# Attention 1 of a two-layer gated block: the exponentials become TensorE's weights, and the maxima a row of the score product that DMA fills

## Chip, cores and metric

One Trainium2 chip, one core. The time is device microseconds of one launch of the whole program, both layers; the runs before gave 1577.19 us (median of three, 1576.49 to 1578.75). Times inside a launch are from one profiled execution, counted from the start of its span. Engines are called as in the profile: PE (TensorE matmuls), PEld (its weight loads), DVE, ACT (ScalarE), POOL (GpSimd), SP (the engine that issues most DMAs).

## What is computed

Two layers, each of a gated attention and a gated feed-forward, on x of 16 x 128 tokens of 256 features. The change is in the second layer's attention ("attention 1"), 32 query heads and 8 groups of keys and values, 8 features a head:

```python
q = (Q @ w_q.T).reshape(B, S, G, HG, HD)
k = (K @ w_k.T).reshape(B, S, G, HD)
v = (V @ w_v.T).reshape(B, S, G, HD)
scores = jnp.einsum('bnghd,bmgd->bnghm', q, k) / scale
scores = jnp.where(pad, NEG_INF, scores)
scores = jnp.where(causal, scores, NEG_INF)
attn = jax.nn.softmax(scores, axis=-1)
out = jnp.einsum('bnghm,bmgd->bnghd', attn, v).reshape(B, S, D)
return out @ w_o.T + b_o
```

x gets tanh(g) times this, and then a mixture of 8 experts follows, whose router reads the result.

## The kernel before

The stages follow each other on all engines: attention 0, feed-forward 0, attention 1, experts. No program sets the order at run time: each engine runs its own list in order, written out by hand with semaphores between the lists.

In feed-forward 0 the keys, values and queries of attention 1 are made beside the main work. Queries and keys are split into three bf16 parts each and sent to DRAM (qsc, ksc); SP loads them back into Q6 and K6 so that 8 features x 6 products of parts lie in 48 rows (two such halves, from row 0 and from row 64, for two heads at once). SP loads K6 early, and Q6 in 48 DMAs of 128 KB, twelve for each quarter of the tokens, at the start of attention 1 (L1468). Values go to VS, each split into an upper and a lower part with a column of ones (18 columns a group): ACT rounds them to VR, DVE takes the difference, POOL copies the upper part.

Attention 1 runs over 16 blocks of 128 tokens, and in each over 4 turns of 2 groups (8 heads): 64 turns i, in a loop over n in which every engine does its part of several turns. In one turn:

- Raw scores (`pe_raw`, L1489 and L1493): two matmuls put the mask into PA, eight add the scores of one bf16 part, tokens on the partitions. DVE takes the maximum over the keys (L1670), 8 numbers a token.
- Shifted scores (`pe_shifted_1`): eight matmuls put the negative maxima into PO by a product with the negative unit matrix (L1503), four of 48 rows and 256 columns add the exact scores (L1510), now with the keys on the partitions.
- ACT takes the exponential (L1623) into P1, POOL clears what lies above the diagonal (L1769), ACT rounds P1 to fp32r (L1629, `act_upper`), DVE takes the rest (L1674, `dve_lower`).
- Weighing (`pe_weigh_1`): four matmuls of 512 columns, with the padded values VP (filled by POOL, L1764) as weights and the exponentials as the moving side, two for each of upper and rest (L1527, L1528); features come out on the partitions.
- Every other turn ACT evicts the sum (L1633), PE turns it to tokens (L1543), DVE adds the parts and divides by the sum of the ones (`dve_normalise`). Once a block PE turns the output (L1549), ACT evicts it (L1639), PE projects it (L1557), DVE adds it to x (L1694, L1699).

For the first 12 blocks, later in the same loop, the router's input is turned (L1574), copied by ACT (L1643) and multiplied with the router's weights (L1582: two matmuls a block, 128x128 fp32 weights, 8 columns). DVE and POOL compute the norms for it at the turns in NEXT, and SP stores the rows (`sp_next_rows`, L1455). At n = 40 SP clears 2 MB of DRAM (eout, L1473). After the loop come the last four blocks' router products, and then the experts (DVE L1995 is their first step).

The order of a turn in PE's list, which decides what waits behind what:

```python
if 0 <= n - 2 < N1:
    pe_shifted_1(pe, n - 2)
if 0 <= n - 4 < N1:
    pe_weigh_1(pe, n - 4)
b = every(n, 4, 11, NB)
if b is not None:
    pe_out_proj(pe, b)
if n < N1:
    pe_raw(pe, n)
```

Of the kernel before, what the change touches and what calls it, by code (L numbers as in the profile page):

```python
# [17 lines left out]
NB = 16  # L18
S = 128
H = 256  # L20
# [46 lines left out]
def build(nc, x, xctxT, maskT, maskrow, small, wqT, wqxT, wkT, wvT, wkvT, smooth, wprojT, gateT, upT, downT, downs,  # L67
# [3 lines left out]
    with ctx:  # L71
# [833 lines left out]
        def pool_attention_0(p):  # L905
# [65 lines left out]
        VS = sb("VS", [128, NB, G, 18])  # L971
# [29 lines left out]
        VR = [sb(f"VR{i}", [128, 256], FR) for i in range(2)]  # L1001
# [15 lines left out]
        s_kk, s_kv, s_ka, s_kr, s_kl, s_kvr, s_klo, s_kvs, s_ks, s_kg = (  # L1017
            sem(n) for n in ("kk", "kv", "ka", "kr", "kl", "kvr", "klo", "kvs", "ks", "kg"))
# [17 lines left out]
        def sp_feed_forward_0(sp):  # L1036
# [65 lines left out]
        def pe_keys_values(pe, q4):  # L1102
# [4 lines left out]
            if q4:  # L1107
                pe.wait_ge(s_kr, q4)
                pe.wait_ge(s_klo, q4)
# [16 lines left out]
        def pe_query_turn(pe, q4):  # L1126
            pe.wait_ge(s_lnorm, layer_norm_count(2, q4))
            if q4 == 0:
                pe.wait_ge(s_kr, 4)
                pe.wait_ge(s_klo, 4)  # L1130
# [57 lines left out]
        def act_keys_values(a, q4):  # L1188
# [8 lines left out]
            if q4 >= 2:  # L1197
                a.wait_ge(s_kvs, q4 - 1)
                a.wait_ge(s_klo, q4 - 1)
            a.activation(VR[q4 % 2][:], PAh[1][:, 0:256], ACT.Copy).then_inc(s_kvr, 1)  # L1200
# [67 lines left out]
        def dve_keys_values(v, q4):  # L1268
            ks = KS[q4 % 2]
            v.wait_ge(s_ka, 2 * q4 + 1)  # L1270
            v.tensor_tensor(RK, PAh[0][0:64, :], ks[:, 0, :], ALU.subtract).then_inc(s_kr, 1)
            v.wait_ge(s_ka, 2 * q4 + 2)
            v.tensor_tensor(ks[:, 2, :], RK, ks[:, 1, :], ALU.subtract).then_inc(s_kl, 1)
            v.wait_ge(s_kvr, q4 + 1)
            if q4 == 0:
                v.wait_ge(s_vone, 2)
            v.tensor_tensor(VS[:, 4 * q4:4 * q4 + 4, :, 9:17], PAh[1][:, 0:256].rearrange("p (b g d) -> p b g d", g=G, d=8),
                            VR[q4 % 2][:].rearrange("p (b g d) -> p b g d", g=G, d=8), ALU.subtract).then_inc(s_klo, 1)
# [91 lines left out]
        def pool_values_upper(p, q4):  # L1370
            p.wait_ge(s_kvr, q4 + 1)
            p.tensor_copy(VS[:, 4 * q4:4 * q4 + 4, :, 0:8], VR[q4 % 2][:].rearrange("p (b g d) -> p b g d", g=G, d=8)).then_inc(
                s_kvs, 1)

# [4 lines left out]
        def pool_feed_forward_0(p):  # L1379
# [4 lines left out]
            for z in range(2):  # L1384
                p.memset(VS[:, :, :, 8 + 9 * z:9 + 9 * z], 1.0 - z).then_inc(s_vone, 1)
# [4 lines left out]
            for q4 in range(4):  # L1390
                pool_values_upper(p, q4)
# [16 lines left out]
        VP = [sb(f"VP{i}", [128, 9, 128], FR) for i in range(2)]  # L1408
        OTS = [sb(f"OTS{i}", [128, 512]) for i in range(2)]
        AO = [sb(f"AO{i}", [128, H]) for i in range(2)]  # L1410
        AOT = sb("AOT", [128, 2, 128])
        OS = sb("OS", [128, 4, 4, 9])
        rl = sb("rl", [128, 4, 4])
        P1 = [sb(f"P1{i}", [128, 1024]) for i in range(2)]
        PH1 = [sb(f"PE1{i}", [128, 2, 512], FR) for i in range(2)]
        PL1 = [sb(f"PL1{i}", [128, 2, 512], FR) for i in range(2)]
        mx1 = [sb(f"mxb{i}", [128, 8], BF16) for i in range(2)]
# [3 lines left out]
        TR = [SS, PC]  # L1421
# [5 lines left out]

        s_wog = sem("wog")
        s_qg = [sem(f"qg{i}") for i in range(4)]
        s_vpz, s_vp, s_sel, s_hi, s_lo, s_ot1, s_oe = (sem(n) for n in ("vpz", "vp", "sel", "hi", "lo", "ot1", "oe"))  # L1430
# [6 lines left out]
        NEXT = {23: 0, 39: 1, 55: 2, 67: 3, 71: 4}  # L1437
# [18 lines left out]

        def sp_attention_1(sp):
# [12 lines left out]
            for n in range(N1 + 14):  # L1470
                if n == 40:
# [7 lines left out]
        def pe_raw(pe, i):  # L1479
            b, g0, tok_ = heads_at(i)  # L1480
            if i == 0:
                pe.wait_ge(s_mask, 1)
                pe.wait_ge(s_kg, 16 * 2 * NP)
# [12 lines left out]

        def pe_shifted_1(pe, i):
            b, g0, tok_ = heads_at(i)
            pe.wait_ge(s_mx, N + i + 1)
            if i:  # L1500
                pe.wait_ge(s_ex, N + i)
            for n in range(8):
                pe.matmul(STB[:, 128 * n:128 * n + 128], mx1[i % 2][:, n:n + 1].broadcast_to([128, 128]), negib[:],  # L1503
                          start=n % 4 == 0, stop=False)
            for half in range(2):
                r = slice(64 * half, 64 * half + 8 * NP)
                for g2 in range(2):
                    g = g0 + g2
                    o = 512 * half + 256 * g2
                    t = pe.matmul(STB[:, o:o + 256], K6[r, g, tok_], Q6[r, 2 * g:2 * g + 2, tok_], start=False, stop=g2 == 1)  # L1510
# [20 lines left out]
        def pe_turn_1(pe, u):  # L1531
            b = u // 2
            pe.wait_ge(s_rt, N + u + 1)
            if u % 2 == 0 and b:
                pe.wait_ge(s_oe, b)
            if u % 2 and b:
                pe.wait_ge(s_add, N + b)
            if u % 2 and b >= 5:
                pe.wait_ge(s_lg, b - 4)
            for j in range(4):  # L1540
                pp, half = divmod(j, 2)
                o = 256 * half + 128 * pp
                t = pe.transpose(TR[u % 2][:, 128 * j:128 * j + 128], OTS[u % 2][:, o:o + 128], identf[:])  # L1543
            t.then_inc(s_T2, 1)

        def pe_out_turn(pe, b):
            pe.wait_ge(s_y0, N + 2 * b + 2)
            for c in range(2):
                t = pe.transpose(TR[0][:, 128 * c:128 * c + 128], AO[b % 2][:, 128 * c:128 * c + 128], identf[:])  # L1549
            t.then_inc(s_ot1, 1)  # L1550

        def pe_out_proj(pe, b):
            pe.wait_ge(s_oe, b + 1)
            if b == 0:
                pe.wait_ge(s_wog, 32)
            for c in range(2):
                t = pe.matmul(TR[1][:, 0:H], AOT[:, c, :], WO[:, c, :], start=c == 0, stop=c == 1)  # L1557
            t.then_inc(s_C, 1)

        def next_bank(b):  # L1560
            return (PAh[0], PAh[1], POa, POb)[b - 12] if b >= 12 else TR[1]
# [23 lines left out]
        def pe_attention_1(pe):  # L1585
            after_feed_forward_0(pe)
            for n in range(N1 + 14):
                b = every(n, 4, 29, NB - 4)
                if b is not None:
                    pe_logits(pe, b)  # L1590
                b = every(n, 4, 10, NB)
                if b is not None:
                    pe_out_turn(pe, b)
                u = every(n, 2, 7, 2 * NB)
                if u is not None:
                    pe_turn_1(pe, u)
                if 0 <= n - 2 < N1:
                    pe_shifted_1(pe, n - 2)
                if 0 <= n - 4 < N1:
                    pe_weigh_1(pe, n - 4)  # L1600
                b = every(n, 4, 11, NB)
# [4 lines left out]
                b = every(n, 4, 28, NB - 4)  # L1606
# [7 lines left out]

        def act_expo_1(a, i):
# [5 lines left out]
            if i >= 2:  # L1621
                a.wait_ge(s_lo, i - 1)
            a.activation(P1[i % 2][:], STB, ACT.Exp, bias=mcf[:, b:b + 1], scale=SC1).then_inc(s_ex, 1)  # L1623

        def act_upper(a, i):
            a.wait_ge(s_sel, i + 1)
            if i >= 2:
                a.wait_ge(s_LO, N + i - 1)
            a.activation(PH1[i % 2][:].rearrange("p a n -> p (a n)"), P1[i % 2][:], ACT.Copy).then_inc(s_hi, 1)  # L1629

        def act_evac_out(a, u):
            a.wait_ge(s_LO, N + 2 * u + 2)
            a.activation(OTS[u % 2][:], OT[u % 2][:], ACT.Copy).then_inc(s_rt, 1)  # L1633

        def act_out_turn(a, b):
# [3 lines left out]
            a.activation(AOT[:].rearrange("p c n -> p (c n)"), TR[0][:, 0:256], ACT.Copy).then_inc(s_oe, 1)  # L1639
# [6 lines left out]
        def act_attention_1(a):  # L1646
            after_feed_forward_0(a)
            for n in range(N1 + 14):
                u = every(n, 2, 6, 2 * NB)
                if u is not None:  # L1650
                    act_evac_out(a, u)
                b = every(n, 4, 10, NB)
                if b is not None:
                    act_out_turn(a, b)
                if 0 <= n - 3 < N1:
                    act_upper(a, n - 3)
                if 0 <= n - 2 < N1:
                    act_expo_1(a, n - 2)
                b = every(n, 4, 28, NB - 4)
# [6 lines left out]
        def dve_maximum_1(v, i):  # L1666
            v.wait_ge(s_S, N + i + 1)
            if i >= 2:
                v.wait_ge(s_ST, N + i - 1)
            v.tensor_reduce(mx1[i % 2][:], PA[:].rearrange("p (j m) -> p j m", m=128), AX, ALU.max).then_inc(s_mx, 1)  # L1670

        def dve_lower(v, i):
            v.wait_ge(s_hi, i + 1)
            v.tensor_tensor(PL1[i % 2][:].rearrange("p a n -> p (a n)"), P1[i % 2][:],  # L1674
# [563 lines left out]
```

## Time and profile before

| | us |
|---|---|
| median of the runs | 1577.19 |
| the profiled execution's own time | 1575.72 |
| its span | 1574.0 |
| TensorE busy in it | 1366.4 (87%) |
| DVE busy | 1215.8 (77%) |
| ACT busy | 1018.8 (65%) |
| POOL busy | 853.1 (54%) |

The mean granted clock of TensorE is 0.957 of full speed. Busy times are sums over the whole span, and each stage has a limit of its own; for a change in one stage the views are cut to that stage: the chain of waits tells which engine's work ended the waiting, the timeline how long a step takes from its start to the start of the next (matmuls overlap, so the busy time of a step is longer than its share), and the windows tell the granted clock and the DMA share of a stretch.

### The profile page before, as it was taken

The page shows a single profiled execution, that of the slowest core. Times are in us where ns is not written, and L with a number is a line of the kernel's source. Part 1 is how long each engine was busy: PE and PEld are TensorE (multiplying, and loading weights), DVE is VectorE, ACT ScalarE, POOL GpSimd, SP SyncE. Part 2 cuts the span into 40 slices and gives each one's busy share as a digit, 9 for nine tenths or more (in the row PEclk, how much of TensorE's full clock was granted, in tenths as well). Part 3 has the DMA queues.
Part 4 walks back from the last instruction along what each step waited for, and adds up shares of the span by engine and source line. Part 5 has one row for each costly group of instructions (what it writes and reads, how often), then busy time and mean ns, then how long its engine had stood idle before and what let it go on. Part 6 is the DMA issues. An engine that isn't in the chain of part 4 may idle for free. (4 is left out here: it accounts for less than half of the span.)

```text
span 1574.0 us, 30371 instructions
## 1 busy us (share of the span) xinstructions
PE 1366.4 (87%) x11712; PEld 1173.5 (75%) x11712; DVE 1215.8 (77%) x2318; ACT 1018.8 (65%) x2168; POOL 853.1 (54%) x912
## 2 busy tenths in 40 slices
PE   0356999999999999999999996999769898994995
PEld 0356899999999999999999985676536555553995
DVE  7999888888888888888888797633448988886554
ACT  4687677877777777778777774312136665652773
POOL 2688767667677676676775464101114433341673
PEclk9999999999999999999999998999979998995997
DMA  3100000000100000001001002340254002003563
GB/s 102 37 24 28 15 22 15 15 21 15 35 15 14 22 15 15 22 15 35 3 14 51 2 1 78 77 62 21 57 97 74 15 1 68 1 15 132 182 216 127
DMA packets 62239, 69.85 MB, mean 44 GB/s; under 512 B 5424, under 2 KB 54800, under 8 KB 61968
## 3 DMA queue, kind: packets, MB, share of 16 engines
q1 hardware_dynamic: 59488, 60.54, 14.6%
q0 software_dynamic: 2432, 7.34, 1.4%
q8 instruction: 93, 1.52, 0.4%
q14 instruction: 50, 0.41, 0.1%
q10 hardware_dynamic: 176, 0.04, 0.0%
HBM read 55.56 MB, written 12.34 MB: 43 GB/s over the span
## 5 line engine op out<-in xcount | busy, mean ns | idle before, releaser
L903 POOL TENSOR_TENSOR RB<-YS,M 128x512 bf16<-128x512 f32 x128 | 151.8, 1186 | 180.3 <-DVE YS L753 180.3
L579 ACT ACTIVATE QT<-B,sm 128x256 f32<-128x256 f32 x256 | 130.4, 560 | 163.8 <-PE B L435 163.8
L1769 POOL TENSOR_SCALAR_AFFINE_SELECT P<-P 128x1024 f32<-128x1024 f32 x64 | 82.1, 1282 | 154.7 <-ACT P L1623 154.7
L455 PE MATMUL SS<-QT,KT 128*128 128x256 f32 x512 | 154.8, 397 | 11.4 <-DVE mx L714 11.3
L892 POOL TENSOR_TENSOR yy<-vv,half 128x12 f32<-128x12 f32 x64 | 147.8, 2310 | 5.3
L403 PE MATMUL PA<-WH,XQ 128*128 128x256 f32 x512 | 140.2, 305 | 7.0 <-ACT SQ L608 7.0
L733 DVE TENSOR_TENSOR QN<-QN,yy 128x512 f32<-128x512 f32 x128 | 134.1, 1048 | 1.7 <-POOL yy L892 1.5
L714 DVE TENSOR_REDUCE mx<-SS 128x4 bf16<-128x512 f32 x128 | 88.2, 689 | 60.7 <-PE SS L447 59.7
L405 PE MATMUL PA<-WL,XQ 128*128 128x256 f32 x512 | 128.8, 283 | 0.0
L726 DVE TENSOR_REDUCE vv<-SQ 128x6 f32<-128x768 f32 x128 | 120.6, 942 | 0.0
L435 PE MATMUL B<-identf,QN 128*128 128x128 f32 x768 | 105.5, 274 | 6.4 <-ACT LNT L534 6.4
L1629 ACT ACTIVATE PE<-P 128x1024 fp32r<-128x1024 f32 x64 | 67.7, 1058 | 65.1 <-POOL P L1769 65.1
L423 PE MATMUL PA<-W,XB 128*128 128x128 bf16 x1536 | 109.2, 221 | 0.4 <-POOL XB L833 0.4
L403 PEld LDWEIGHTS PA<-WH,XQ 128*128 128x128 f32 x512 | 98.6, 193 | 7.6 <-ACT SQ L608 7.6
L471 PE MATMUL PO<-V,PPP 128*128 128x129 f32 x512 | 98.9, 275 | 5.2 <-DVE Y L741 5.2
L582 ACT ACTIVATE KT<-B,sm 128x128 f32<-128x128 f32 x256 | 103.1, 460 | 0.0
L471 PE MATMUL PO<-VR,PPP 128*128 128x129 f32 x512 | 99.0, 275 | 0.0
L405 PEld LDWEIGHTS PA<-WL,XQ 128*128 128x128 f32 x512 | 98.8, 193 | 0.0
L899 POOL TENSOR_TENSOR VR<-V,RSM 128x256 f32<-128x256 f32 x128 | 96.6, 754 | 0.0
L489 PE MATMUL PC<-PH,RT 128*128 128x256 f32 x512 | 92.0, 301 | 3.1 <-ACT RT L600 2.8
L435 PEld LDWEIGHTS B<-identf,QN 128*128 128x128 f32 x768 | 88.5, 141 | 6.6 <-issue 6.6
L753 DVE SCALAR_TENSOR_TENSOR YS<-Y,M 128x512 f32<-128x512 bf16 x128 | 89.3, 697 | 4.4
(331 smaller groups left out, 4516.1 us busy)
## 6 DMA issues: line engine op xcount, KB each, us to landing
W<-in_w SPq DMA_DIRECT2D x16, 1024.0 KB
Q<-qsc SPq DMA_DIRECT2D x48, 128.0 KB
WR<-in_wprojT SPq DMA_DIRECT2D x16, 256.0 KB, 3.0
K<-ksc SPq DMA_DIRECT2D x12, 256.0 KB
qsc<-T POOLq DMA_DIRECT2D x8, 384.0 KB, 4.2
X<-in_x SPq DMA_DIRECT2D x4, 512.0 KB, 5.9
CR<-in_xctxT SPq DMA_DIRECT2D x8, 256.0 KB, 2.8
RSM<-rsm_d SPq DMA_DIRECT2D x16, 128.0 KB, 4.1
```

The source lines that it names most:

```text
L403: pe.matmul(PA[:, 256 * k:256 * k + 256], XQ[:, k, c, bs], wh[:, c, 256 * k:256 * k + 256], start=c == 0, stop=False)
L405: t = pe.matmul(PA[:, 256 * k:256 * k + 256], XQ[:, k, c, bs], wl[:, c, 256 * k:256 * k + 256], start=False, stop=c == 1)
L423: t = pe.matmul(PA[:, 768 + 128 * k:896 + 128 * k], XB[:, k, c, bs], wb[:, c, part, 128 * k:128 * k + 128], start=c == 0 and part == 0, st ...
L435: t = pe.transpose(dst, QN[i % 4][:, 128 * h:128 * h + 128], identf[:])
L455: pe.matmul(SS[:, 256 * z:256 * z + 256], k[:, 128 * z:128 * z + 128], q[:, 256 * z:256 * z + 256], start=True, stop=False)
L471: t = pe.matmul(PO[:, z, 129 * j:129 * j + 129], p[:, 128 * h:128 * h + 128], v[j][:, 1 - z, :], start=True, stop=True)
L579: a.activation(QT[i % 2][:, o:o + 256], B1[:, o:o + 256], ACT.Identity, bias=col(n + "b"), scale=col(n + "w"))
L582: t = a.activation(KT[i % 2][:, o:o + 128], B2[:, o:o + 128], ACT.Identity, bias=col(n + "b"), scale=col(n + "w"))
L726: v.tensor_reduce(w_[:, 6 * h:6 * h + 6], SQ[:].rearrange("p (h d) -> p h d", d=128), AX, ALU.add).then_inc(s_red, 1)
L733: v.tensor_tensor(q[:, 0:4], q[:, 0:4], y[:, 6 * h:6 * h + 4].unsqueeze(2).broadcast_to([128, 4, 128]), ALU.mult).then_inc(s_mul, 1)
L892: p.tensor_tensor(yy[j % 2][:], v_, half[:], ALU.pow).then_inc(s_rstd, 1)
L903: p.tensor_tensor(RB[i % 2][:], YS[:], M[:], ALU.subtract).then_inc(s_rb, 1)
```

## The change

- The maxima of the four turns of a block are kept together (mxb, 32 columns); one matmul turns and negates them (`pe_max_turn`), ACT copies them to MT, and two DMAs of SP write them into row 48 of each half of Q6 (`sp_maxima`). Row 48 of K6 holds ones, written in feed-forward 0 by two DMAs. The shifted scores are now four matmuls of 49 rows, without the eight of L1503.
- The exponentials stay fp32, are not split, and are the weights of the weighing: eight matmuls a turn, each with 128x128 fp32 weights and 9 columns of values (8 features and the ones). They give the output by tokens, so the eviction and turns of L1633 and L1543 go; DVE divides straight from PSUM, once a block.
- The values are not split: ACT writes them to VS; the difference on DVE and the copies on POOL go, and so do VP and its clearing.
- P1 has three buffers. Turns are drawn apart: shifted scores of turn i come 7 turns of the loop after its raw scores (2 before), the weighing 2 after that; the output, router and norm steps move 4 turns later.

```diff
         def sp_feed_forward_0(sp):
...
             sp.wait_ge(s_ks, 64)
+            sp.wait_ge(s_vone, 2)
             for half in range(2):
+                sp.dma_start(K6[64 * half + 48:64 * half + 49, :, :].rearrange("o g (b t) -> o (g b) t", t=128),
+                             ones1[:]).then_inc(s_kg, 16)
...
-        NEXT = {23: 0, 39: 1, 55: 2, 67: 3, 71: 4}
+        NEXT = {27: 0, 43: 1, 59: 2, 71: 3, 75: 4}
...
+        def sp_maxima(sp, b):
+            sp.wait_ge(s_mte, b + 1)
+            for half in range(2):
+                sp.dma_start(Q6[64 * half + 48:64 * half + 49, :, 128 * b:128 * b + 128],
+                             MT[b % 2][16 * half:16 * half + 16, :]).then_inc(s_mr[b % 2], 16)
...
         def sp_attention_1(sp):
...
                         sp.dma_start(Q6[r0:r0 + 8, :, 512 * q4:512 * q4 + 512], src[:, :, 512 * q4:512 * q4 + 512]).then_inc(
                             s_qg[q4], 16)
             for n in range(N1 + 14):
+                b = every(n, 4, 5, NB)
+                if b is not None:
+                    sp_maxima(sp, b)
...
+        def pe_max_turn(pe, b):
+            pe.wait_ge(s_mx, N + 4 * b + 4)
+            if b:
+                pe.wait_ge(s_mte, b)
+            if b >= 3:
+                pe.wait_ge(s_oe, b - 2)
+            pe.matmul(SS[0:32, 256:384], mxb[b % 2][:], negib[:], start=True, stop=True).then_inc(s_mt, 1)
...
         def pe_shifted_1(pe, i):
             b, g0, tok_ = heads_at(i)
-            pe.wait_ge(s_mx, N + i + 1)
+            if i % 4 == 0:
+                pe.wait_ge(s_mr[b % 2], 32 * (b // 2 + 1))
             if i:
                 pe.wait_ge(s_ex, N + i)
-            for n in range(8):
-                pe.matmul(STB[:, 128 * n:128 * n + 128], mx1[i % 2][:, n:n + 1].broadcast_to([128, 128]), negib[:],
-                          start=n % 4 == 0, stop=False)
             for half in range(2):
-                r = slice(64 * half, 64 * half + 8 * NP)
+                r = slice(64 * half, 64 * half + 8 * NP + 1)
...
         def pe_weigh_1(pe, i):
             b, g0, tok_ = heads_at(i)
-            u = i // 2
-            ps_ = OT[u % 2]
-            vp = VP[b % 2][:].rearrange("p g n -> p (g n)")
-            pe.wait_ge(s_lo, i + 1)
-            if i % 4 == 0:
-                pe.wait_ge(s_vp, b + 1)
-            if u >= 2 and i % 2 == 0:
-                pe.wait_ge(s_rt, N + u - 1)
-            for g2 in range(2):
+            pe.wait_ge(s_sel, i + 1)
+            if i % 4 == 0 and b >= 2:
+                pe.wait_ge(s_y0, N + b - 1)
+            for n in range(8):
+                half, g2, pp = n // 4, n // 2 % 2, n % 2
                 g = g0 + g2
-                o = 128 * (g + 1) - 32 * (g % 4)
-                n = slice(256 * g2, 256 * g2 + 256)
-                pe.matmul(ps_[:], vp[:, o:o + 128], PH1[i % 2][:, :, n], start=g % 4 == 0, stop=False)
-                t = pe.matmul(ps_[:], vp[:, o:o + 128], PL1[i % 2][:, :, n], start=False, stop=g % 4 == 3)
+                o = 9 * (4 * g + 2 * pp + half)
+                t = pe.matmul(OT[b % 2][:, o:o + 9], P1[i % 3][:, 128 * n:128 * n + 128], VS[:, b, g, :], start=True, stop=True)
             t.then_inc(s_LO, 1)
...
         def pe_attention_1(pe):
             after_feed_forward_0(pe)
             for n in range(N1 + 14):
...
+                b = every(n, 4, 5, NB)
+                if b is not None:
+                    pe_max_turn(pe, b)
+                if 0 <= n - 7 < N1:
+                    pe_shifted_1(pe, n - 7)
+                if 0 <= n - 9 < N1:
+                    pe_weigh_1(pe, n - 9)
...
         def act_expo_1(a, i):
...
-            if i >= 2:
-                a.wait_ge(s_lo, i - 1)
-            a.activation(P1[i % 2][:], STB, ACT.Exp, bias=mcf[:, b:b + 1], scale=SC1).then_inc(s_ex, 1)
+            if i >= 3:
+                a.wait_ge(s_LO, N + i - 2)
+            a.activation(P1[i % 3][:], STB, ACT.Exp, bias=mcf[:, b:b + 1], scale=SC1).then_inc(s_ex, 1)
...
-        def act_upper(a, i):
...
-        def act_evac_out(a, u):
...
-        def dve_lower(v, i):
...
-        def pool_values(p, b):
...
```

## Rows read from the trace of the kernel before

**Rows 1.** The page's first line.

```profile
span 1574.0 us, 30371 instructions
```

**Rows 2.** Timeline, PE, stage ends: start us, us, what, [idle before <-releaser].

```profile
1155.85 1.01 PE L1489 MATMUL PA<-MS,identb 128*128 128x512 bf16 x2 [10.28 <-DMA Q<-qsc]
...
1158.76 1.04 PE L1489 MATMUL PA<-MS,identb 128*128 128x512 bf16 x2 [1.34 <-DVE mxb L1670]
...
1160.27 1.03 PE L1503 MATMUL PO<-negib,mxb 128*128 128x128 bf16 x8
1161.24 0.61 PE L1510 MATMUL PO<-Q,K 48*128 48x256 bf16 x4
1161.78 1.04 PE L1489 MATMUL PA<-MS,identb 128*128 128x512 bf16 x2
...
1436.64 1.83 PEld L1582 LDWEIGHTS PA<-WG,ZX 128*128 128x128 f32 x8
1438.36 1.83 PEld L1582 LDWEIGHTS PO<-WG,ZX 128*128 128x128 f32 x8
```

**Rows 3.** The same, the last weighing matmul and the experts' first step.

```profile
1419.72 0.40 PE L1528 MATMUL B<-PL,VP 128*128 128x512 f32 x1
...
1440.52 0.29 DVE L1995 TENSOR_REDUCE rm<-LG 128x16 f32<-128x128 f32 x1
```

**Rows 4.** Windows, mid-stage: stretch, us, busy (count) by engine, PEclk, DMA share, GB/s.

```profile
1212.00:1421.00 209.00, 183.90 (x1504) 116.46 (x1502) 172.82 (x287) 124.78 (x148) 79.78 (x104) 0.94 0.06 19
```

**Rows 5.** Chain that ended last, in order of time: start us, us, what.

```profile
1196.70 1.10 ACT P L1623
...
1197.86 1.34 POOL P L1769
...
1199.25 0.94 issue
1200.19 1.10 ACT P L1623
```

**Rows 6.** Timeline of PE in mid-stage, at a granted clock of 1.00.

```profile
1282.45 0.60 PE L1489 MATMUL PA<-MS,identb 128*128 128x512 bf16 x2
...
1283.33 0.66 PE L1543 MATMUL SS<-identf,OTS 128*128 128x128 f32 x4
...
1284.37 0.40 PE L1510 MATMUL PO<-Q,K 48*128 48x256 bf16 x4
1284.69 0.50 PE L1527 MATMUL B<-PE,VP 128*128 128x512 f32 x1
...
1285.72 1.03 PE L1557 MATMUL PC<-WO,AOT 128*128 128x256 f32 x4
...
1291.19 0.61 PE L1582 MATMUL PC<-WG,ZX 128*128 128x8 f32 x4 [0.47 <-ACT ZX L1643]
```

**Rows 7.** Groups, 1155 to 1425: xcount | busy us, mean ns | idle before.

```profile
L1670 DVE TENSOR_REDUCE mxb<-PA 128x8 bf16<-128x1024 f32 x64 | 78.1, 1220 | 18.2 <-PE PA L1493 17.5
```

**Rows 8.** SP issues in the timeline; a window; a DMA with us to landing.

```profile
1127.95 75.89 SPq L1468 DMA_DIRECT2D Q<-qsc  x48
...
1210.00:1212.00 2.00, 1.74 (x15) 0.78 (x14) 2.00 (x3) 1.48 (x2) 0.45 (x1) 1.00 0.19 47
...
WG<-in_wgate SPq DMA_DIRECT2D x1, 8.0 KB, 2.9
```

**Rows 9.** Timeline of the weight loads, one block's router product.

```profile
1291.19 0.52 PEld L1582 LDWEIGHTS PC<-WG,ZX 128*128 128x128 f32 x4 [0.71 <-ACT ZX L1643]
```

**Rows 10.** Windows (columns as in rows 4), four stretches of attention 1.

```profile
1158.00:1170.00 12.00, 9.90 (x68) 4.81 (x69) 5.54 (x6) 5.58 (x6) 2.49 (x3) 0.50 0.56 88
1170.00:1180.00 10.00, 10.00 (x86) 5.78 (x84) 8.07 (x10) 6.76 (x8) 3.44 (x3) 0.94 0.56 71
1436.60:1440.30 3.70, 3.68 (x18) 3.58 (x17) 0.50 (x3) 0.64 (x2) 0.00 (x0) 0.50 0.12 40
...
1240.00:1260.00 20.00, 15.44 (x134) 9.41 (x134) 17.58 (x25) 10.14 (x13) 10.66 (x18) 1.00 0.08 27
```

More of the change, by code:

```diff
@@ L1383, in pool_feed_forward_0 @@
             pool_parts(p, 1)
-            for z in range(2):
-                p.memset(VS[:, :, :, 8 + 9 * z:9 + 9 * z], 1.0 - z).then_inc(s_vone, 1)
+            p.memset(VS[:, :, :, 8:9], 1.0).then_inc(s_vone, 1)
+            p.memset(ones1[:], 1.0).then_inc(s_vone, 1)
             p.memset(caus[:], 0.0).then_inc(*ps.up())
@@ L1407, in build @@
         WG = sb("WG", [128, 2, E])
-        VP = [sb(f"VP{i}", [128, 9, 128], FR) for i in range(2)]
-        OTS = [sb(f"OTS{i}", [128, 512]) for i in range(2)]
         AO = [sb(f"AO{i}", [128, H]) for i in range(2)]
         AOT = sb("AOT", [128, 2, 128])
[L1412 to L1417, printed above, removed]
+        rl = sb("rl", [128, 32])
+        P1 = [sb(f"P1{i}", [128, 1024]) for i in range(3)]
+        mxb = [sb(f"mxb{i}", [128, 32], BF16) for i in range(2)]
+        MT = [sb(f"MT{i}", [32, 128], BF16) for i in range(2)]
         ti = sb("ti", [128, 128], I32)
@@ L1429, in build @@
         s_qg = [sem(f"qg{i}") for i in range(4)]
[L1430 removed]
+        s_sel, s_ot1, s_oe = (sem(n) for n in ("sel", "ot1", "oe"))
+        s_mt, s_mte = sem("mt"), sem("mte")
+        s_mr = [sem("mr0"), sem("mr1")]
         s_nt, s_xt, s_lgp, s_lg, s_zr = (sem(n) for n in ("nt", "xt", "lgp", "lg", "zr"))
@@ L1509, in pe_shifted_1 @@
                     o = 512 * half + 256 * g2
-                    t = pe.matmul(STB[:, o:o + 256], K6[r, g, tok_], Q6[r, 2 * g:2 * g + 2, tok_], start=False, stop=g2 == 1)
+                    t = pe.matmul(STB[:, o:o + 256], K6[r, g, tok_], Q6[r, 2 * g:2 * g + 2, tok_], start=True, stop=True)
             t.then_inc(s_ST, 1)
@@ L1555, in pe_out_proj @@
                 pe.wait_ge(s_wog, 32)
+            else:
+                pe.wait_ge(s_add, N + b)
+            if b >= 5:
+                pe.wait_ge(s_lg, b - 4)
             for c in range(2):
-                t = pe.matmul(TR[1][:, 0:H], AOT[:, c, :], WO[:, c, :], start=c == 0, stop=c == 1)
+                t = pe.matmul(PC[:, 0:H], AOT[:, c, :], WO[:, c, :], start=c == 0, stop=c == 1)
             t.then_inc(s_C, 1)
         def next_bank(b):
-            return (PAh[0], PAh[1], POa, POb)[b - 12] if b >= 12 else TR[1]
+            return (PAh[0], PAh[1], POa, POb)[b - 12] if b >= 12 else PC
         def pe_next_turn(pe, b):
@@ L1587, in pe_attention_1 @@
             for n in range(N1 + 14):
-                b = every(n, 4, 29, NB - 4)
+                b = every(n, 4, 33, NB - 4)
                 if b is not None:
                     pe_logits(pe, b)
-                b = every(n, 4, 10, NB)
+                b = every(n, 4, 14, NB)
                 if b is not None:
                     pe_out_turn(pe, b)
[L1594 to L1601, printed above, removed]
+                b = every(n, 4, 5, NB)
[5 more added lines that the diff above has]
+                    pe_weigh_1(pe, n - 9)
+                b = every(n, 4, 15, NB)
                 if b is not None:
@@ L1605, in pe_attention_1 @@
                     pe_raw(pe, n)
-                b = every(n, 4, 28, NB - 4)
+                b = every(n, 4, 32, NB - 4)
                 if b is not None:
@@ L1648, in act_attention_1 @@
             for n in range(N1 + 14):
[L1649 to L1652, printed above, removed]
+                b = every(n, 4, 5, NB)
+                if b is not None:
+                    act_max_turned(a, b)
+                b = every(n, 4, 14, NB)
                 if b is not None:
                     act_out_turn(a, b)
[L1655 to L1659, printed above, removed]
+                if 0 <= n - 7 < N1:
+                    act_expo_1(a, n - 7)
+                b = every(n, 4, 32, NB - 4)
                 if b is not None:
@@ L1735, in dve_attention_1 @@
                     dve_routing_constants(v)
-                b = every(n, 4, 29, NB - 4)
+                b = every(n, 4, 33, NB - 4)
                 if b is not None:
                     dve_logits(v, b)
-                u = every(n, 2, 7, 2 * NB)
-                if u is not None:
-                    dve_normalise(v, u)
-                if 0 <= n - 3 < N1:
-                    dve_lower(v, n - 3)
-                b = every(n, 4, 11, NB)
+                b = every(n, 4, 13, NB)
+                if b is not None:
+                    dve_normalise(v, b)
+                b = every(n, 4, 15, NB)
                 if b is not None:
@@ L1787, in pool_attention_1 @@
                     pool_routing_constants(p)
-                b = every(n, 4, 0, NB)
-                if b is not None:
-                    pool_values(p, b)
-                if 0 <= n - 2 < N1:
-                    pool_select(p, n - 2)
+                if 0 <= n - 7 < N1:
+                    pool_select(p, n - 7)
                 if n in NEXT and NEXT[n] <= 2:
@@ L1826, in build @@
         who = (B2[:, 0:3 * E], PC[:, 0:3 * E])
-        s_slots, s_sub, s_exp, s_oh, s_A, s_who, s_idx, s_wgt = (
-            sem(n) for n in ("slots", "sub", "exp", "oh", "A", "who", "idx", "wgt"))
+        s_slots, s_sub, s_exp, s_oh, s_A, s_who, s_idx, s_wgt, s_hi = (
+            sem(n) for n in ("slots", "sub", "exp", "oh", "A", "who", "idx", "wgt", "hi"))
         s_e = [sem("e0"), sem("e1")]
```

117 lines of the change are left out of this document (38 added, 79 removed).

## The prediction

> **What bounds the kernel now.** I read the page's head first [rows 1]: the profiled execution has a span of 1574.0 us and a time of 1575.72, so 1.7 us lie around the span; the median of the runs, 1577.19, is 1.5 above it. The change touches attention 1, which runs from 1155.85 (the first score matmul, held back by the Q loads) [rows 2] to 1440.5, where the experts begin [rows 3]. In its middle TensorE is busy for 183.90 of 209 us at a granted clock of 0.94 [rows 4]: nearly full, but the chain of waits [rows 5] shows who sets the pace. An exponential (1.10) ends, POOL's causal select (1.34) follows, then ScalarE's rounding copy, in front of the next exponential in its program, holds that back for another 0.94 (the chain calls it "issue"). From exponential to exponential that is 3.49 us (1196.70 to 1200.19), 64 times. The last weighing matmul ends at 1420.1; the tail to the experts takes 20.4 us [rows 3].
>
> **What goes.** The rounding copy leaves ScalarE, the subtraction leaves DVE, and PE loses the eight matmuls that put the maxima into the scores, the four weighing matmuls (1.03 us, 1284.69 to 1285.72) and the turns of L1543, 0.66 us every other turn [rows 6]. The 3.49 us chain is gone: exponential and select now lie between a score matmul and a weighing two turns later, so at least 2 x 3 us of PE work cover their 2.5 us. DVE keeps one maximum of 1.22 us a turn [rows 7], covered by the 2.2 us of PE work that stand between one raw score and the next. What replaces the chain is PE's own sum and the way of the maxima through DMA.
>
> **The preparation** in feed-forward 0 loses casts and subtractions and gains two DMAs of ones, issued with the K loads, long ahead of their use; the gate and up matmuls, which PE runs meanwhile, cover both, and the clearing of VP falls into the wait for the Q loads. If that cover were gone it would be a few copies. I take 0, with bounds of 2 us either way.
>
> **The first maxima.** SP issues 48 Q loads first, from 1127.95 without a break for 75.89 us, thus until 1203.84; the maxima's DMAs stand behind them in SP's program and in its queue, whose data runs on: the share of the DMA engines is still 0.19 in 1210 to 1212 [rows 8]. Before, the first shifted score started at 1160.27 [rows 2]. Now PE does seven raw scores (n = 0 to 6, done by about 1176 at the 2.91 us from 1155.85 to 1158.76) and waits at shifted score 0. If the small transfers overtook the Q data, they would land at 1203.84 + 2.9 (the nearest small one, 8 KB) = 1207; if they wait behind it, at 1212 or up to 2.9 later. I take 1212.5: the queue is the same. Later maxima have two turns (6 us or more) for a ScalarE copy, two issues and such a landing; only b = 9, behind the 2 MB clearing of eout, could be late, by 0 to 3 us once. I take 0. SP's other waits come after the maxima of their turn.
>
> **PE's sum at full clock.** Raw scores 0.88 (1282.45 to 1283.33), shifted scores 0.32 (1284.37 to 1284.69; the 49th row adds no column) [rows 6]. The weighing is new: eight matmuls of fp32 weights with nine columns. Its nearest relative is the router product, 128x8 with fp32 weights: two matmuls of the program give four records, each with its own weight load, and the four loads take 0.52 together [rows 9], 0.13 each with the first one's beginning; half of the step at half clock (0.215, below) is 0.11, which I take. So 16 loads: 16 x 0.11 and 0.12 to begin = 1.9 us a turn, bound by the loads. From shifted score 0 to the last weighing: 64 x (0.32 + 1.9) = 142; 57 raw scores x 0.88 = 50; 16 x (output turn 0.3, half of L1543's; maxima 0.1, an estimate from one matmul of 128 columns; projection 0.9 of the 1.03 shown, whose end the next covers) = 21; 12 blocks of router work x 1.4 (turn 0.3, wait 0.47, logits 0.61) = 17 [rows 6]. Sum 230.
>
> **PE's sum at half clock.** At the granted clock of 0.50 (1.2 GHz instead of 2.4) the raw scores took 1.51 (1158.76 to 1160.27), the shifted ones 0.54 (1161.24 to 1161.78), and eight such loads start 1.72 after the eight before, a step of 0.215 [rows 2]: 16 x 0.215 + 0.2 = 3.6. 64 x (0.54 + 3.6) = 265; 57 x 1.51 = 86; the rest at twice the full price or a little less, 16 x 2.5 and 12 x 2.0, 64. Sum 415.
>
> **Which of the two.** After the long wait PE begins at half clock. Rows show that being busy does not bring the full clock by itself: from 1158 to 1170 PE was busy 9.90 of 12 us with raw, maxima and shifted scores and stayed at 0.50, and from 1436.6 to 1440.3 it was busy 3.68 of 3.70 with weight loads and eight-column matmuls, the very form of the new weighing, and stayed at 0.50 [rows 10]. In the first stretch the clock rose only after the 512-column weighing matmuls had joined (0.94 from 1170 on); the change takes those and the maxima matmuls away and fills their place with loads. So I take half clock almost throughout, with short rises where the projection (four records of 256 columns) and raw scores stand together, some 8% of the way: 415 - 0.08 x 185 = 400 us. The bounds are 230 and 415.
>
> The page "TensorE: Matmul & The Clock Gate" of the Trainium skill ("Why this matters for your kernels") says that an engine kept continuously busy with matmuls gets the full rate. By that rule the sum would be 230 instead of 400, the first rival below; the stretch at 1436.6, busy without gaps at 0.50, speaks against it.
>
> **The sum.** 1212.5 + 400 = 1612.5 for the last weighing. Tail: 20.4 less an eviction and two small DVE steps, which are gone: 18, bounds 16 and 21. Experts unchanged: 1574.0 - 1440.5 = 133.5. Span 1764, time 1765.7, and with the 1.5 of the median 1767: slower by 190 us, of which 52 lie before shifted score 0 (1212.5 instead of 1160.3), part of them won back by the seven raw scores done ahead.
>
> **Rivals.** (A) The clock comes back and stays: PE is never idle after 1212.5. For it: 1240 to 1260 shows 1.00 although PE was busy only 15.44 of 20 us [rows 10]. Against it: the rows at 0.50 above, and PE starts from 0.50. It gives 1212.5 + 230 + 18 + 133.5 + 3.2 = 1597, slower by 20, since the wait for the maxima isn't won back. (B) It comes and goes: raised at each projection and held for a turn or more, so that a third to a half of the work runs at full clock. With 415 - 0.33 x 185 = 354 to 415 - 0.5 x 185 = 322 it gives 1721 to 1690. (C) Faster: at full clock the weight loads overlap each other, so that the weighing is bound by something shorter. At the step of the bf16 matmuls of 128 columns (eight between 1160.27 and 1161.24 [rows 2], 0.12 each at half clock, so 0.06 at full) 16 records take 1.1 with their beginning instead of 1.9: 64 x 0.8 = 51 less, 1546. It decides from the point where PE's way is under 1420.1 - 1212.5 + 2.4 = 210 us, that is, a step under 0.09. Against it: four loads in a row at 0.13 or a little less, with nothing else to wait for [rows 9], and it needs the full clock too. That the maxima's row does not do its work has no sign in the diff: the row of ones in K6 and the negative maxima in Q6 are both there.
>
> **How the numbers follow.** Half clock 0.72, A 0.12, B 0.12, C 0.03, and 0.01 for no change. The likeliest gives 1767; its own range is 1735 (rises for a quarter of the way) to 1790 (no rise, latest landing, late transfers). The range reaches down through B, to 1685, and up to 1795; A and C are left out with 0.16. A measurement here tells about 0.2%, 3 us, from no change. Faster 0.03, same 0.01, slower 0.96.
>
> **What would show it.** In the trace after: PE idle until about 1212 with shifted score 0 released by the DMA of the maxima; 16 weight loads a turn at a step of 0.21 (right) or 0.11 (A); the granted clock near 0.50 in attention 1; exponentials 6 us apart or more, with ScalarE, DVE and POOL idle most of the time; the router's start near 1630. It would be wrong if the first shifted score started before 1200, or if the clock stood at 1.00 in the middle of the stage.

## The result, and the profile after

The median of four runs went from 1577.97 to 1743.68 us. One of the four of the changed kernel, 1763.04, was in a slower state with a lower granted clock, so the ratio, 1.1014 (95% interval 1.0976 to 1.1052), and all differences between medians below leave such runs out; the median of the other three is 1739.61. The prediction was 1767, with a range of 1685 to 1795. The profiled run took 1747.76 us, the slowest of these three.

The page of the changed kernel first: its span, the granted clock over 40 slices, and the groups of attention 1 (busy us, mean ns, idle before).

```profile
span 1745.7 us, 30282 instructions
...
PEclk9889999999999999999999899955555555555798
...
L1525 PEld LDWEIGHTS B<-VS,P 128*128 128x128 f32 x1024 | 215.1, 319 | 24.8 <-issue 24.6
L1729 POOL TENSOR_SCALAR_AFFINE_SELECT P<-P 128x1024 f32<-128x1024 f32 x64 | 69.9, 1094 | 329.5 <-ACT P L1618 329.5
L1525 PE MATMUL B<-VS,P 128*128 128x9 f32 x1024 | 220.7, 355 | 0.0
...
L1654 DVE TENSOR_REDUCE mxb<-PA 128x8 bf16<-128x1024 f32 x64 | 78.3, 1224 | 222.1 <-PE PA L1490 222.1
...
L1618 ACT ACTIVATE P<-PO,mcf 128x1024 f32<-128x1024 f32 x64 | 71.2, 1113 | 166.6 <-PE PO L1513 166.6
```

DVE and ScalarE now wait for TensorE, and POOL for ScalarE's exponential (222, 167 and 330 us idle ahead of their main steps), and the clock line has a run of fives where attention 1 lies. The windows show it closer (stretch, us, busy by engine, PEclk, DMA share, GB/s).

```profile
1160.00:1180.00 20.00, 8.69 (x60) 2.81 (x59) 7.34 (x6) 0.27 (x1) 0.00 (x0) 0.50 0.55 101
1180.00:1200.00 20.00, 0.00 (x0) 0.00 (x0) 0.00 (x0) 0.00 (x0) 0.00 (x0) 0.50 0.56 110
...
1240.00:1300.00 60.00, 60.00 (x310) 43.03 (x311) 16.14 (x20) 11.80 (x14) 9.82 (x9) 0.50 0.00 1
1300.00:1350.00 50.00, 49.19 (x264) 35.98 (x264) 17.61 (x32) 10.83 (x13) 12.07 (x21) 0.53 0.04 11
1350.00:1450.00 100.00, 98.11 (x502) 71.33 (x502) 28.90 (x54) 20.83 (x27) 19.91 (x34) 0.50 0.09 27
1450.00:1550.00 100.00, 96.93 (x539) 70.74 (x540) 30.13 (x51) 21.94 (x28) 19.85 (x28) 0.57 0.02 6
```

From 1180 to 1200 nothing computes; from 1240 to 1300 TensorE is busy without a gap and has half its clock. The timeline gives the steps behind both.

```profile
1150.40 42.18 SPq L1462 DMA_DIRECT2D Q<-qsc  x30
1156.01 1.01 PE L1486 MATMUL PA<-MS,identb 128*128 128x512 bf16 x2 [10.81 <-DMA Q<-qsc]
...
1175.22 1.22 DVE L1654 TENSOR_REDUCE mxb<-PA 128x8 bf16<-128x1024 f32 x1 [1.70 <-PE PA L1490]
1192.62 17.57 SPq L1448 DMA_DIRECT2D Q<-MT  x4
1203.19 0.61 PE L1513 MATMUL PO<-Q,K 49*128 49x256 bf16 x4 [28.03 <-DMA Q<-MT]
...
1240.81 1.01 PE L1486 MATMUL PA<-MS,identb 128*128 128x512 bf16 x2
...
1242.30 0.61 PE L1513 MATMUL PO<-Q,K 49*128 49x256 bf16 x4
1242.84 3.58 PE L1525 MATMUL B<-VS,P 128*128 128x9 f32 x16
1246.27 2.05 PE L1546 MATMUL PC<-WO,AOT 128*128 128x256 f32 x4
...
1454.09 1.95 PE L1525 MATMUL B<-VS,P 128*128 128x9 f32 x16
1455.90 0.59 PE L1486 MATMUL PA<-MS,identb 128*128 128x512 bf16 x2
...
1592.49 3.42 PE L1525 MATMUL B<-VS,P 128*128 128x9 f32 x16
...
1610.92 0.29 DVE L1952 TENSOR_REDUCE rm<-LG 128x16 f32<-128x128 f32 x1
```

Seven raw scores are done at 1175; the first shifted score starts at 1203.19, after 28.03 us of idle time that the maxima's DMA ends (before: 1160.27 [rows 2]). A weighing takes 3.43 us (1242.84 to 1246.27), a plain turn 5.46. At 1454 the clock is up for a moment, and the same sixteen records take 1.81.

Where the 171.7 us of span come from: the first shifted score is 42.9 later; from it to the last weighing's end it takes 392.7 (1203.19 to 1595.91) in place of 259.8 (1160.27 to 1420.1 [rows 2, 3]), 132.9 more; the tail is 5.4 shorter (15.0), the experts 1.3 longer.

### The profile page after: what moved, and what is told of

The parts are those of the page before. It is cut to its first block and busy times, and to the rows that moved or that the text cites. A ratio compares the mean times of both kernels' runs of the same rounds, so it can differ in the third digit from the quotient of the medians.

```text
span 1745.7 us, 30282 instructions
## 1 busy us (share of the span) xinstructions
PE 1530.3 (88%) x11856; PEld 1318.9 (76%) x11856; DVE 1112.1 (64%) x2152; ACT 945.1 (54%) x2088; POOL 828.5 (47%) x892
## 5 line engine op out<-in xcount | busy, mean ns | idle before, releaser
L1525 PEld LDWEIGHTS B<-VS,P 128*128 128x128 f32 x1024 | 215.1, 319 | 24.8 <-issue 24.6
L1729 POOL TENSOR_SCALAR_AFFINE_SELECT P<-P 128x1024 f32<-128x1024 f32 x64 | 69.9, 1094 | 329.5 <-ACT P L1618 329.5
L1525 PE MATMUL B<-VS,P 128*128 128x9 f32 x1024 | 220.7, 355 | 0.0
L1654 DVE TENSOR_REDUCE mxb<-PA 128x8 bf16<-128x1024 f32 x64 | 78.3, 1224 | 222.1 <-PE PA L1490 222.1
L1618 ACT ACTIVATE P<-PO,mcf 128x1024 f32<-128x1024 f32 x64 | 71.2, 1113 | 166.6 <-PE PO L1513 166.6
```

The source lines that it names most:

```text
L1525: t = pe.matmul(OT[b % 2][:, o:o + 9], P1[i % 3][:, 128 * n:128 * n + 128], VS[:, b, g, :], start=True, stop=True)
```

## The experiments

The theory: two costs that add. The maxima stand behind 48 query loads on SP, and the new weighing leaves TensorE at half clock. Times are medians; ratios are to the kernel before, run beside each. In the cuts of code "..." stands for lines left out.

**Query loads interleaved with the maxima** (`sp_queries` issues the twelve loads of one quarter).

```diff
-            for q4 in range(4):
...
+            sp_queries(sp, 0)
             for n in range(N1 + 14):
                 b = every(n, 4, 5, NB)
                 if b is not None:
                     sp_maxima(sp, b)
+                    if b < 3:
+                        sp_queries(sp, b + 1)
```

> Only the order of SP's issues is changed: the query loads of the second, third and fourth quarter go out behind the maxima of blocks 0, 1 and 2, not ahead of them. Theory (two costs that add: TensorE idles 28 us for the first maxima, which stand behind 48 query loads on SP; and the new weighing then leaves it at half clock): the first shifted score comes right behind the seventh raw score, at about 1177 us in place of 1203, the granted clock stays 0.50 for most of the stage, and the time falls by about 26 us, from 1744 to about 1718. Rival (the idle stretch is what puts the clock at half, and a stage without it would run up): the clock rises to 1.00 and the time is near 1580. Second rival (the wait only moves to the first turn of the second quarter, which now waits for its loads): no change, 1744.

Measured: 1726.36, ratio 1.0968 (1.0929 to 1.1008), 13 us less than the changed kernel, half of the expected 26; the clock stayed at 0.50 from 1240 to 1300. Its timeline:

```profile
1167.83 8.34 SPq L1457 DMA_DIRECT2D Q<-qsc  x12
...
1171.72 0.61 PE L1517 MATMUL PO<-Q,K 49*128 49x256 bf16 x4
...
1197.28 0.61 PE L1517 MATMUL PO<-Q,K 49*128 49x256 bf16 x4 [8.50 <-DMA Q<-MT]
```

The first shifted score comes at 1171.72, without a wait, 31.5 us sooner. Block 1's maxima now stand behind the twelve loads of the second quarter, and TensorE waits 8.50 us for them: the second rival, in part. The profiled spans differ by 24.3. So the order on SP is the cause of the long wait, and the idle stretch isn't what sets the clock.

**The maxima's DMAs issued by ACT.**

```diff
+            a.wait_ge(s_mte, b + 1)
+            for half in range(2):
+                a.dma_start(Q6[64 * half + 48:64 * half + 49, :, 128 * b:128 * b + 128],
+                            MT[b % 2][16 * half:16 * half + 16, :]).then_inc(s_mr[b % 2], 16)
```

> The query loads stay in their order; only the two DMAs of each block's maxima are issued by ACT, behind its own copy, in place of SP. Theory (the 28 us come from SP's order, in which the maxima stand behind 48 query loads): the maxima of block 0 go out at about 1170 us, the first shifted score comes at about 1177 in place of 1203, with no later wait for block 1, and the time falls by 24 to 28 us to about 1718. Rival (what holds the maxima is the transfers themselves, since both share the 16 DMA engines): they are issued early and land when the query loads are through, the first shifted score stays at 1195 to 1203 and the time at 1735 to 1744.

Measured: 1719.51, ratio 1.0888 (1.0852 to 1.0924), 20 us less, or 28.6 between the profiled spans. Its timeline:

```profile
1167.69 22.11 SPq L1462 DMA_DIRECT2D Q<-qsc  x20
...
1169.13 1.24 ACTq L1608 DMA_DIRECT2D Q<-MT  x2
...
1177.28 0.61 PE L1510 MATMUL PO<-Q,K 49*128 49x256 bf16 x4 [2.92 <-DMA Q<-MT]
```

The maxima go out 23.5 us sooner, while some twenty query loads are still to be issued, and release the score 8.2 us later: 2.92 us idle in place of 28.03. What held the maxima was their place on SP. The loads beside them still cost something: from issue to landing the maxima took up to 7.5 us here, up to 9.4 behind the loads on SP, and 1.7 and 1.8 in the medians over all blocks. So nearly all of the gain is the earlier issue. The page "DMA: Bandwidth & Descriptors" of the Trainium skill ("Queues, rings and completion order") says that SP and ACT own separate queue rows, between which a DMA engine takes turns. The separate rows agree with this run; the turns it doesn't show, since the landing is little shorter than behind the loads.

**Weighing over 112 columns.**

```diff
-                t = pe.matmul(OT[b % 2][:, o:o + 9], P1[i % 3][:, 128 * n:128 * n + 128], VS[:, b, g, :], start=True, stop=True)
+                c = 72 * b + 9 * g
+                w = min(112, 72 * NB - c)
+                t = pe.matmul(OT[b % 2][:, o:o + w], P1[i % 3][:, 128 * n:128 * n + 128], vs_[:, c:c + w], start=True, stop=True)
```

> The weighing's eight matmuls a turn go over 112 columns in place of 9: the same weights, the same loads, the same results in the 9 columns that are read; the other columns are overwritten by the next heads or lie past the 288 that are read. Theory (the clock stays at half because the weighing shows TensorE nine columns between two loads of fp32 weights): the granted clock goes to 1.00 for most of the stage, the weighing takes about 1.8 to 2.0 us a turn, as in the short rises of the changed kernel, a turn about 3.1 us, and the time falls from 1744 to about 1600 (1585 to 1625); the start's wait of 28 us stays. Rival (the clock is at half for another reason, such as the idle start or the loads themselves, and the columns don't matter): the clock stays 0.50 and the time is 1744 or, where the columns outlast the loads, longer, up to 1780.

Measured: 1618.54, ratio 1.0271 (1.0242 to 1.03), 121 us less. Windows and a turn from its timeline:

```profile
1200.00:1220.00 20.00, 13.97 (x79) 9.02 (x80) 3.67 (x3) 6.00 (x6) 4.37 (x4) 0.50 0.09 17
1220.00:1240.00 20.00, 20.00 (x190) 15.09 (x190) 8.86 (x10) 7.28 (x8) 6.18 (x6) 1.00 0.01 1
1240.00:1300.00 60.00, 57.96 (x524) 43.06 (x522) 31.19 (x48) 20.62 (x25) 20.13 (x29) 0.97 0.03 11
```

```profile
1220.04 0.60 PE L1486 MATMUL PA<-MS,identb 128*128 128x512 bf16 x2
...
1221.23 2.04 PE L1529 MATMUL B<-VS,P 128*128 128x112 f32 x16
1223.11 0.60 PE L1486 MATMUL PA<-MS,identb 128*128 128x512 bf16 x2
```

The same weights and loads (their order by heads changed too, which wasn't tried alone), with columns that nobody reads, and the clock goes to 1.00 some 15 us after the first shifted score (1204.97). The weighing takes 1.88 us, hardly more than the 1.81 of the nine columns at full clock: the loads set its length either way. A turn falls from 5.46 to 3.07 us. This is the larger cost, and it is the clock's.

**A burst ahead of the first shifted score.**

```diff
+            if i == 0:
+                for _ in range(24):
+                    pe.matmul(STB[:, 0:512], identb[:], MS[:, 0, :].unsqueeze(1).broadcast_to([128, 4, 128]), start=True, stop=True)
```

> Ahead of the first shifted score, behind its wait, TensorE does 24 more bf16 matmuls of 512 columns into the bank that the score then overwrites; nothing else is changed. Theory (it is the steady stream of weighings that the chip answers with half clock): the clock rises in or behind the burst and is back at 0.50 within a few turns, and the time is 1744 plus 5 to 10 us for the burst less at most 2.4 us for each turn at full clock, 1740 to 1755. Rival (the stage only starts low, after 28 us of idle, and would hold full clock once raised): the clock stays 1.00 to the end and the time is about 1595 to 1610.

Measured: 1747.6, ratio 1.1088 (1.1029 to 1.1146), 8 us more. Its timeline:

```profile
1198.35 7.25 PE L1508 MATMUL PO<-MS,identb 128*128 128x512 bf16 x24 [24.87 <-DMA Q<-MT]
1205.54 0.40 PE L1516 MATMUL PO<-Q,K 49*128 49x256 bf16 x4
...
1208.51 0.40 PE L1516 MATMUL PO<-Q,K 49*128 49x256 bf16 x4 [1.70 <-ACT P L1621]
1208.84 0.86 PE L1486 MATMUL PA<-MS,identb 128*128 128x512 bf16 x2
...
1210.93 3.58 PE L1528 MATMUL B<-VS,P 128*128 128x9 f32 x16
```

The burst brings full clock (0.40 for a shifted score), and it is gone in the second raw score, 0.86, ahead of the first weighing, 3.58. TensorE had waited 1.70 us for the first exponential between; from there on it is busy without a gap (1220 to 1300), and the clock stays at 0.50. So a raised clock isn't held. Whether the wait or the work behind it took the clock away, this run doesn't tell, as it was gone before any weighing; the next run shows a fall without a wait.

**The maxima by matmuls again, the new weighing kept.** Where the 49th row was, eight matmuls of `mxb` columns against `negib` as in the kernel before; no turn, copy or DMA of maxima.

> The change's other half alone is undone: the maxima enter the score product by eight 128-column bf16 matmuls a turn, as in the kernel before, with 48 rows of queries and keys; no turn of the maxima and no DMA of them (their columns lie in three buffers, so that the lag of seven turns holds). The weighing by fp32 weights over 9 columns stays. Theory: the start's wait of 28 us goes, and eight matmuls a turn come, some 0.9 us at half clock (0.5 at full). If the weighing alone decides the clock it stays at 0.50 and the time is 1744 - 28 + 64 x 0.9 = about 1770 (1750 to 1785). Rival (the 1024 bf16 columns that come back each turn are enough for the clock to rise): 1.00 for most of the stage, a turn near 3.6 us, and a time of about 1744 - 28 - 64 x 1.9 = 1595.

Measured: 1765.3, ratio 1.1176 (1.1144 to 1.1209). Its windows, one stretch, and a rise in its timeline:

```profile
1240.00:1300.00 60.00, 60.00 (x356) 44.74 (x356) 14.21 (x17) 10.79 (x11) 9.89 (x10) 0.53 0.00 1
```

```profile
1251.40 0.62 PE L1506 MATMUL PO<-negib,mxb 128*128 128x128 bf16 x8
...
1252.28 1.95 PE L1525 MATMUL B<-VS,P 128*128 128x9 f32 x16
...
1255.08 1.03 PE L1506 MATMUL PO<-negib,mxb 128*128 128x128 bf16 x8
```

The 1024 bf16 columns that come back each turn hardly raise the clock. It rises behind a projection (at 1248), stays up for one weighing, and falls (0.62 to 1.03 for the same eight matmuls) with no idle time between. So the halves of the change part: the new weighing, with its order of turns, makes the kernel 12% slower, and the maxima's row takes 26 us of that back although its first DMA stalls TensorE for 28.

**Both costs away: 112 columns, and two query loads a turn between the maxima.**

```diff
+                k = 2 * (n - 5)
+                if 0 <= k < 36:
+                    sp.wait_ge(s_mx, N + n + 1)
+                    sp_queries(sp, 1 + k // 12, range(k % 12, k % 12 + 2))
```

> Both costs taken away at once: the weighing goes over 112 columns, and SP issues only the first quarter's query loads ahead of the loop, then each block's maxima in their place, and two query loads a turn between them. Theory (the two costs are separate and add): the first shifted score at about 1172 us, the granted clock 1.00 from some 15 us behind it, and the profiled span of the run with 112 columns alone (1608.0) falls by 31 us to about 1577, the time to 1575 to 1590, level with the kernel before. Rival (they are not separate: with the loads running beside the scores, the DMAs or TensorE are slower, or a late query load stops TensorE): 1595 to 1615.

Measured: 1592.9, ratio 1.0079 (1.0049 to 1.011), outside the expected 1575 to 1590. Its timeline, then its windows:

```profile
1172.86 9.39 SPq L1457 DMA_DIRECT2D Q<-qsc  x8
...
1182.29 1.14 SPq L1448 DMA_DIRECT2D Q<-MT  x2
...
1192.93 0.61 PE L1519 MATMUL PO<-Q,K 49*128 49x256 bf16 x4 [4.32 <-DMA Q<-MT]
```

```profile
1212.00:1400.00 188.00, 172.80 (x1426) 130.51 (x1424) 79.29 (x130) 58.40 (x73) 53.86 (x75) 0.90 0.17 31
```

The maxima of block 1 are issued behind eight loads and release their score 10.6 us later: TensorE still waits for maxima behind the few loads ahead of them, from 1190 to 1425 for 16.5 us in all, and the clock is 0.90 (0.94 with 112 columns alone). That is the rival's case, with maxima late and not query loads.

**The same with a burst ahead of the first raw score** (24 matmuls as above, while the first query loads land).

> As the run with both costs taken away, and in the idle time ahead of the first raw score, while the first quarter's query loads land, TensorE does 24 bf16 matmuls of 512 columns into a bank that the first raw score overwrites. Theory: the idle time of 6 to 10 us covers most of the 24, the clock is at 1.00 when the raw scores start and stays there, each of the first seven raw turns takes about 2.3 in place of 2.92 us and the first turns behind them 3.1 in place of 5.5, so 5 to 15 us less than the run with both: 1565 to 1580. Rival (the clock falls back in the first raw turns, which are idle for nearly half of their time): no difference from that run, or some us more where the 24 outlast the idle time.

Measured: 1596.86, ratio 1.0106 (1.0078 to 1.0133): no gain. Its timeline:

```profile
1159.17 0.60 PE L1494 MATMUL PA<-MS,identb 128*128 128x512 bf16 x2 [1.34 <-DVE mxb L1666]
...
1161.46 1.04 PE L1494 MATMUL PA<-MS,identb 128*128 128x512 bf16 x2 [1.34 <-DVE mxb L1666]
```

The rival held: three raw turns run at full clock, the fourth is at half again.

**112 columns and ACT's queue.**

> The run with the maxima's DMAs issued by ACT and the run with 112 columns together: query loads in their first order and at full speed ahead of the scores, no wait for block 1, weighing over 112 columns. Theory (two separate costs, and the paced order gave some of its gain back in later waits and slower turns): the run with 112 columns alone, 1618.5 us, less the 24 us that ACT's queue brought, 1594, or somewhat less: 1585 to 1598. Rival (the costs are not separate): no better than the paced run, 1593 to 1610.

Measured: 1576.53, ratio 0.9992 (0.9962 to 1.0022): the kernel before's time, and 22 us better than the two gains added. Its windows:

```profile
1212.00:1400.00 188.00, 178.81 (x1603) 134.66 (x1602) 92.44 (x158) 65.13 (x82) 61.55 (x92) 0.98 0.07 21
```

The first shifted score starts at 1180.33, 24.6 us sooner than with 112 columns alone, as ACT's queue promised. From there to the end of the last weighing it takes 243.8 in place of 252.2 us, and the clock goes with that: 0.98 here, 0.94 there in the same stretch. Another 7 us are in no trace, since the profiled spans differ by 35 and the medians by 42. Its own runs lie between 1566.94 and 1589.58; why the clock falls once more or once less isn't settled.

**The mask's matmuls left out as well.**

```diff
-            for half in range(2):
-                pe.matmul(PAh[half], identb[:], MS[:, b, :].unsqueeze(1).broadcast_to([128, 4, 128]), start=True, stop=False)
...
-                              start=False, stop=n % 4 == 3)
+                              start=True, stop=True)
```

> As the run with ACT's queue and 112 columns, and the two 512-column bf16 matmuls that put the mask into each raw score are left out: the maxima then go over all 128 keys of the block, hidden ones too; the hidden ones still get no weight, since the select and the exponential's bias stay. Theory (TensorE is the bound of the changed stage, so what it no longer does is gained): 0.53 us a turn at full clock, 64 turns, 34 us: about 1558 (1550 to 1575), faster than the kernel before. Rival (these 1024 columns a turn are among those that hold the clock up): the clock falls in a good part of the stage, and the time is 1594 to 1660.

Measured: 1562.79, ratio 0.9893 (0.9844 to 0.9942), 14 us less than with the mask, and 1.1% faster than the kernel before, which wasn't run without its mask. A turn of its timeline, and a window:

```profile
1288.26 0.41 PE L1485 MATMUL PA<-K,Q 8*128 8x128 bf16 x8
...
1290.89 0.41 PE L1485 MATMUL PA<-K,Q 8*128 8x128 bf16 x8
```

```profile
1240.00:1400.00 160.00, 148.15 (x1264) 120.26 (x1262) 76.86 (x140) 56.60 (x72) 53.90 (x85) 0.89 0.08 25
```

A turn at full clock is 2.63 in place of 3.07 us, which by itself would bring 64 x 0.44 = 28 us. In the profiled executions the first shifted score comes 6.5 us sooner, and from it to the last weighing, with 57 such turns (25 us), it takes 236.0 in place of 243.8, only 7.8 less. Some 7 us of the rest are longer waits of TensorE (19.6 in place of 12.5); the others go with the clock, 0.89 where the run with the mask has 0.98 in the same stretch. So the theory and the rival both hold in part.

**The first seven raw turns filled** (ACT's queue, 112 columns, with the mask).

```diff
+                if n < 7:
+                    for _ in range(3):
+                        pe.matmul(STB[:, 0:512], identb[:], MS[:, 0, :].unsqueeze(1).broadcast_to([128, 4, 128]), start=True, stop=True)
```

> As the run with ACT's queue and 112 columns, and behind each of the first seven raw scores, where TensorE waits 1.3 us a turn for the maximum, it does three bf16 matmuls of 512 columns into the bank that the first shifted score overwrites. Theory: with no idle time the clock is at 1.00 within the first raw turns and stays there into the weighing; raw turns of 2.3 in place of 2.92 us and two to four weighing turns of 3.1 in place of 5.5 bring 5 to 12 us against the run without them. Rival (the wait of 3 us for the first maxima lets the clock fall anyway): 0 to 3 us.

Measured: 1572.08, ratio 0.9971 (0.9948 to 0.9994), 4.3 us less than without the filling; the two intervals overlap. Its timeline:

```profile
1161.65 0.82 PE L1598 MATMUL PO<-MS,identb 128*128 128x512 bf16 x3
...
1172.93 0.61 PE L1510 MATMUL PO<-Q,K 49*128 49x256 bf16 x4 [3.61 <-DMA Q<-MT]
...
1178.94 3.64 PE L1526 MATMUL B<-VS,P 128*128 128x112 f32 x16
```

Full clock in the raw turns from the third on, half again behind 3.61 us of idle time: mostly the rival.

**Without the mask and with the filling.**

> The run without the mask's matmuls and the run with the first seven raw turns filled, together (ACT's queue and 112 columns in both). Theory (their gains lie in different places, one in every turn, one ahead of the first weighings): 1562.8 us less the 4.5 us that the filling brought, about 1558 (1552 to 1564), faster than the kernel before. Rival (without the mask's columns the clock falls more often, and the filling holds it up only at the start): no different from the run without the filling, 1560 to 1566.

Measured: 1564.3, ratio 0.9885 (0.984 to 0.993): no different from the run without the filling (its interval was 0.9844 to 0.9942), the rival's case.

## Why the prediction was right

- The seven raw scores: "done by about 1176 at the 2.91 us"; they took 2.92 each and ended at 1175. The preparation at 0: the first raw score starts at 1156.01, before at 1155.85.
- The first maxima: the mechanism was right, the size off. "I take 1212.5: the queue is the same" came 9.3 us too late, and left 3 us to a sign of being wrong (a start before 1200). The maxima did wait for the queue, 10.6 us from issue to the score where 8.7 were taken, but SP issued its last query load before 1192.62, not at 1203.84: the loads ran at 101 to 110 GB/s between 1160 and 1200, those before at 71 to 88 [rows 10], at the same DMA share of 0.55 to 0.56. Why is open: from 1180 to 1200, with TensorE busy in both, the run with ACT's queue moved 108 and the one with the maxima by matmuls 79. The later maxima at 0 was right: all 28.0 us of such waits are the first one.
- "So I take half clock almost throughout": right, and shown by the 112 columns to be the weighing's doing. PE's sum was 400, measured 392.7. The weighing was put at 3.6, with 0.2 to begin; it took 3.43, as its beginning lies under the matmuls ahead: 64 x 0.17 = 11 us less, and the other terms together some 4 us more. The rises were right in size: 8% of the work is 18 us at full clock, and the windows at 0.53 and 0.57 hold 3 and 14 us of it, 17 in five rises.
- The window from 1240 to 1300, 60.00 of 60.00 us busy at 0.50, bears out the step that rested on the 3.70 us at 1436.6, which was little to rest it on. The rule of the page "TensorE: Matmul & The Clock Gate" of the Trainium skill ("Why this matters for your kernels"), full rate for continuous work, doesn't hold for this work; the measurement decides.
- Rival B's rises came, but for 17 of 392.7 us only. Rival A (1597) has its form, with the clock back for most of the stage, in the run with 112 columns (1618.54); rival C's condition failed, since at full clock the step was 1.81 / 16 = 0.113, the predicted 0.11.
- The tail was 15.0, not 18, and outside its bounds of 16 and 21; the experts 134.8, not 133.5.

With the measured terms: 1203.2 + 392.7 + 15.0 + 134.8 = 1745.7. The forecast's 1767 is 23 above the median: 9.3 from the maxima, 7.3 from PE's sum, 1.7 from tail and experts together, and 5 because the median was taken 3.2 above the profiled span and lies 2.0 below it.

## What to carry to other kernels

Making the large operand the weights removes evictions and copies, but it can turn TensorE's time into weight loads with a few columns between them; look in the trace for stretches of that form and read the clock they were granted before counting on full speed. Where loads set the pace, wider moving operands cost next to nothing (1.88 against 1.81 us a weighing at full clock) and here brought the clock back. A small DMA that the next step waits for doesn't belong behind bulk loads on the same engine: another engine issued it 23.5 us sooner here, and with 112 columns that gave 1576.53, where spacing the loads gave 1592.9.

## What the runs showed of the hardware that was not expected

- With 1024 more bf16 columns a turn in the scores the stretch from 1240 to 1300 was granted 0.53, with the wider weighing 0.97.
- The query loads moved 71 GB/s in one kernel and 110 in the other at the same DMA share, 0.56.
- POOL's select, with the same shape, takes 1.09 to 1.17 us in the changed kernel; before it took 1.09 to 2.17, with a median of 1.30 (1.34 in [rows 5]). The cause wasn't tested.
- The run with ACT's queue and 112 columns scatters by 1.4%, the kernel before beside it by 0.7%. Its fastest run, 1566.94, had a mean clock of 0.953, its longest, 1589.58, one of 0.944.
